# A macaron block on one core: stage 1's small FFN on token halves, one addition moved to GpSimd, and stage 2 entered without a common stop

## The chip, the cores and the metric

One core of a Trainium2 chip runs the whole program in one launch. The metric is the device time of an execution in microseconds (us); lower is better. The core's engines are named as in the profile: PE (TensorE; PEld are its weight loads), DVE (VectorE), ACT (ScalarE), POOL (GpSimd) and SP (SyncE, which here only issues DMAs). Each engine runs its own instruction list in order, and the lists meet at semaphores.

## The reference, cut to what matters

The input `x` is 8192 tokens of 512 features, in float32. Three sub-blocks follow each other, each behind a layer norm.

```python
x = x + 0.5 * ffn(layernorm(x))        # Win, bin, W1, b1, W2, b2, Wout, bout
x = x + attn(layernorm(x))             # rmsnorm, delta-rule attention, rmsnorm, gelu MLP 512-2048-512
x = x + 0.5 * ffn(layernorm(x))        # the same FFN, the same weights

def ffn(x):                            # 512 features -> 64 channels -> 512 features
    s = einsum('btd,dm->btm', x, Win) + bin_
    h = relu(s[..., None] * W1 + b1)   # each of the 64 channels has 16 units of its own
    g = einsum('btmh,mh->btm', h, W2) + b2
    return einsum('btm,md->btd', g, Wout) + bout
```

The attention has 16 heads of 32 features. It is a recurrence over tokens, which the kernel computes in chunks of 32 tokens (a triangular system in each chunk, then a state carried from chunk to chunk).

## The kernel before, in words

The program has three stages, and all engines pass through them in the same order.

**Stage 1** (`pe_project`, `act_project`, `dve_project`, `pool_project`, `sp_project`) handles 16 tiles of 512 tokens. For a tile t it does the first FFN, both norms, and the projections to q, k, v and beta. PE's list in the loop over t is written out by hand: 13 projections `project(t, 0..12)` (j = 0 is beta; then v, q, k for each of four head groups). Between them stand the products of other tiles: `hidden(t + 1)` (Win), `ffn_out(t + 1)` (Wout), the transposes `turn_x(t + 2)` and `turn_h(t + 1)`, and four `gram` products of k and q, two of them of the tile before. The weights of the projections and both sides of them are split into a high and a low part, so that each product is three matmuls (L236 to L238). The FFN's matmuls are plain float32.

The FFN of tile t + 1 runs through the engines as follows. `hidden` (L371) makes s in one PSUM bank. Win's 64 columns stand twice side by side, so that partitions 0 to 63 and 64 to 127 hold the same s. ACT's `relus` (L520) makes 8 units at a time on both halves (units 0 to 7 on the lower partitions, 8 to 15 on the upper ones), 512 tokens wide, in two buffers. DVE's `sums` (L701 for the first, L705 for the other seven) weighs and adds them into `g1`. `ffn_out` (L380) multiplies by Wout, which also stands twice, and so adds the two halves. It writes the banks 6 and 7 in turn, so that its third and fourth matmul wait until DVE's `add_ffn` (L712) has emptied the bank of the first and second. `add_ffn` adds into X, to which DVE's `add_bout` (L693) had added 0.5 bout. Then come the statistics of the second norm (L717, L724), and ACT's second norm.

`system0` is extra work on DVE (L806, L812) and POOL: the triangular systems of the first 1024 tokens are solved inside stage 1, in four parts that go in at t = 3, 6, 9, 12 and come out at t = 6, 9, 12, 15.

SP issues the loads and the stores of a tile in the order of `sp_project`. The stores of k (L270), beta times k (L274) and of the gram results (L283, L286) of the last tile stand at its end.

**Between stage 1 and stage 2** every engine drains and adds to the semaphore `done1`. SP waits for four of them and for all stores, adds the fifth, and only then do all engines go on. SP then issues the first loads of stage 2: `ringA` and `ringB` for four chunks (L1147, L1152, L1158), Wo in four pieces (L1176), and the second system (L1138).

**Stage 2** (`*_delta`) runs over 256 chunks of 32 tokens. Its matmuls are 32x32 tiles (L1245); every four chunks there is one product with Wo (L1330). PE's code begins with straight lines and goes on with a loop. At chunk 0, ACT splits Wo into high and low parts (L1426) after its first chunk's work, DVE makes the low part (L1526), and both then go on. DVE and POOL solve the systems of the 1024 tokens ahead (L1495, L1499) between their other work, in slots that a function hands out at build time.

**Stage 3** (`*_dense`) does the MLP and the second use of the small FFN. There the small FFN is already worked on token halves: `hidden` (L1728) makes tiles of 64 columns, partitions 0 to 63 holding the first half of the tokens and 64 to 127 the second, 16 ReLUs (L1874) and 16 sums (L2020) are 256 wide, and `ffn_out` (L1739) takes 64 rows at a time.

## Time and profile before

| | us |
|---|---|
| median of 3 runs | 3223.64 (3222.89 to 3228.33) |
| the profiled execution, its own time | 3230.83 |
| its span, first to last instruction | 3228.9 |
| mean granted TensorE clock | 0.979 of full |
| PE busy | 3065.5 (95%) |
| DVE busy | 1933.4 (60%) |
| ACT busy | 1420.3 (44%) |
| POOL busy | 1226.6 (38%) |

Shares of busy time are means over the three stages. In the trace, stage 1's projections begin at 52.7 us, the last matmul of stage 1 ends at 937.7, and the first of stage 2 begins at 948.2; stage 3 begins at about 1711. A float32 matmul of L371, L380, L1728 or L1739 shows as two rows of PE, so 4 of them are "x8". The end of a matmul is modelled, and the next one starts before it: the 128x512 matmuls of a projection last 0.39 us each in the rows and follow each other every 0.227 us.

### The profile page before, as it was taken

Reading aid. Unit: us, or ns where it says so; the run is one execution under the profiler, and the core shown is the slowest. Engines: PE = TensorE matmul, PEld = TensorE weight load, DVE = VectorE, ACT = ScalarE, POOL = GpSimd, SP = SyncE. Lnnn points to the kernel's source line nnn. Section 1 sums busy time; section 2 is a strip of 40 time slices with the busy share of each in tenths; the row PEclk is TensorE's granted clock in tenths of the full one; section 3 lists DMA queues with packets and bytes.
Section 4 is the critical chain, followed back from the end, with each engine's and each line's share of the span. In section 5 each row is a group of like instructions: output and inputs, shape, how many; then the busy total and the mean of one; then the engine's idle time right before and its main releaser. Section 6 shows DMA issues by size and latency. Waiting matters only on the chain.

```text
span 3228.9 us, 148563 instructions
## 1 busy us (share of the span) xinstructions
PE 3065.5 (95%) x67876; PEld 2475.0 (77%) x67876; DVE 1933.4 (60%) x3190; ACT 1420.3 (44%) x3226; POOL 1226.6 (38%) x1225
## 2 busy tenths in 40 slices
PE   5999999999957999999999999999999999999998
PEld 3777677676746888888898777777777777777876
DVE  6787878878738888888613434444444444444434
ACT  5544545444413555554454334434433343444334
POOL 1336565655526776766511211212222121222211
PEclk9999999999967999999999999999999999999999
DMA  3545555555465777776672222222222222222220
GB/s 103 158 145 177 145 158 157 154 156 151 145 202 168 217 217 216 217 217 214 194 212 77 65 66 59 72 78 59 72 66 66 74 57 79 66 66 66 79 66 26
DMA packets 471353, 402.34 MB, mean 125 GB/s; under 512 B 68032, under 2 KB 391744, under 8 KB 471104
## 3 DMA queue, kind: packets, MB, share of 16 engines
q1 hardware_dynamic: 460960, 382.39, 40.4%
q10 hardware_dynamic: 10144, 16.63, 1.7%
q8 instruction: 155, 2.54, 0.3%
q14 instruction: 94, 0.77, 0.1%
HBM read 199.69 MB, written 153.09 MB: 109 GB/s over the span
## 4 chain that ended last, share of the span: by engine, by line
PE 59%; DVE 7%; SPq 2%; issue 2%; DMA 1%; ACT 1%; DVEq 0%; ACTq 0%
PE bank L236 14%; PE bank L238 14%; PE bank L237 14%; PE bank L1245 8%; PE bank L1330 6%; DVE tmp L1495 2%; DVE sysf L1499 2%; PE bank L1739 1%; SPq L1667 1%; PE bank L1728 1%; DVE zb L1518 1%; DVE oT_lo L1512 1%; DVE xt L1483 0%; DMA x2T<-HT 0%; DVE sysf L1474 0%
## 5 line engine op out<-in xcount | busy, mean ns | idle before, releaser
L1985 DVE TENSOR_TENSOR glo<-gl,gh 128x512 fp32r<-128x512 f32 x256 | 205.6, 803 | 715.6 <-ACT gh L1857 713.9
L1853 ACT ACTIVATE gl<-bank,b1m 128x512 f32<-128x512 f32 x256 | 175.8, 687 | 712.3 <-PE bank L238 712.3
L238 PE MATMUL bank<-w_hi,glo 128*128 128x512 f32 x1024 | 404.8, 395 | 0.0
L236 PE MATMUL bank<-h,w_hi 128*128 128x512 f32 x1024 | 403.4, 394 | 0.1
L238 PE MATMUL bank<-h,w_lo 128*128 128x512 f32 x1024 | 403.4, 394 | 0.0
L237 PE MATMUL bank<-w_lo,gh 128*128 128x512 f32 x1024 | 402.7, 393 | 0.0
L237 PE MATMUL bank<-h,w_hi 128*128 128x512 f32 x1024 | 402.2, 393 | 0.0
L236 PE MATMUL bank<-w_hi,gh 128*128 128x512 f32 x1024 | 399.8, 390 | 0.0
L1245 PE MATMUL bank<-ringA 32*32 32x32 f32 x16384 | 344.0, 196 | 15.7 <-issue 7.3
L1245 PEld LDWEIGHTS bank<-ringA 32*32 32x32 f32 x16384 | 271.7, 104 | 11.6 <-DMA ringA<-xt 6.2
L1399 ACT ACTIVATE de<-bank 128x64 f32<-128x64 f32 x512 | 114.5, 224 | 301.3 <-PE bank L1245 296.7
L236 PEld LDWEIGHTS bank<-h,w_hi 128*128 128x128 f32 x1024 | 192.3, 188 | 70.9 <-issue 29.0
L237 PEld LDWEIGHTS bank<-w_lo,gh 128*128 128x128 f32 x1024 | 192.0, 188 | 45.5
L237 PEld LDWEIGHTS bank<-h,w_hi 128*128 128x128 f32 x1024 | 192.2, 188 | 44.7
L236 PEld LDWEIGHTS bank<-w_hi,gh 128*128 128x128 f32 x1024 | 192.4, 188 | 44.0
L238 PEld LDWEIGHTS bank<-w_hi,glo 128*128 128x128 f32 x1024 | 192.0, 188 | 42.1
L238 PEld LDWEIGHTS bank<-h,w_lo 128*128 128x128 f32 x1024 | 192.1, 188 | 41.1
L974 POOL TENSOR_TENSOR nrm<-nrm,cst 128x16 f32<-128x16 f32 x64 | 185.5, 2899 | 94.6 <-DVE nrm L768 94.0
L2139 POOL TENSOR_TENSOR Z<-Z,H 128x512 f32<-128x512 f32 x64 | 92.7, 1448 | 293.5 <-DMA H<-x_scratch 293.5
L1499 DVE TENSOR_TENSOR sysf<-sysf,tmp 128x90 f32<-128x90 f32 (+14 forms) x210 | 195.1, 929 | 4.9
L2147 POOL TENSOR_SCALAR rs<-mv 128x4 f32<-128x4 f32 x15 | 8.5, 570 | 481.4 <-DVE mv L2002 481.4
L1245 PE MATMUL bank<-sT,nR 32*32 32x32 f32 x8192 | 184.1, 198 | 6.5 <-issue 6.5
(195 smaller groups left out, 7288.4 us busy)
## 6 DMA issues: line engine op xcount, KB each, us to landing
ringB<-heads_scratch SPq DMA_DIRECT2D x256, 192.0 KB, 3.3
ringA<-heads_scratch SPq DMA_DIRECT2D x256, 128.0 KB, 2.7
x2T<-HT SPq DMA_DIRECT2D x480, 64.0 KB, 2.0
X<-in_L_attn_x SPq DMA_DIRECT2D x16, 1024.0 KB, 10.0
x_scratch<-X SPq DMA_DIRECT2D x16, 1024.0 KB, 4.5
heads_scratch<-vb SPq DMA_DIRECT2D x16, 1024.0 KB, 5.2
heads_scratch<-qk SPq DMA_DIRECT2D x16, 1024.0 KB, 6.8
heads_scratch<-kb SPq DMA_DIRECT2D x16, 1024.0 KB, 5.2
```

What stands on the lines that cost most here:

```text
L236: e.matmul(o, lhs[0], rhs[0], start=first, stop=False)
L237: e.matmul(o, lhs[0], rhs[1], start=False, stop=False)
L238: return e.matmul(o, lhs[1], rhs[0], start=False, stop=last)
L974: e.tensor_tensor(nrm[:, u], nrm[:, u], pos_half.broadcast_to([P, TC]), ALU.pow).then_inc(o_pow, 1)
L1245: made.append(e.matmul(out[r, n, :], lhsT[r, n, :], rhs[r, n, :], start=first and n == 0, stop=True, skip_group_check=True))
L1330: m = e.matmul(bank[B_WO][:, :], oh[x][:, f, :], wo[y][:, f, :], start=k == 0, stop=k == 11)
L1399: e.activation(heads(de[c % 2][:, 2 * h:2 * h + 2, :]), bank[B_DELTA[h]][:, 0:P // 2], ACT.Copy).then_inc(a_delta[c % 4], 1)
L1495: e.tensor_tensor(tt, N[:, :, j + 1:CH, j:j + 1].broadcast_to([P, 3, rows, j]), N[:, :, j:j + 1, 0:j].broadcast_to([P, 3, rows, j]), ALU.m ...
L1499: e.tensor_tensor(N[:, :, j + 1:CH, 0:j], N[:, :, j + 1:CH, 0:j], tt, ALU.add).then_inc(v_sol, 1)
L1853: e.activation(ordered, made, ACT.Gelu_apprx_tanh, bias=b1m[:, m:m + 1]).then_inc(a_gl, 1)
L1985: e.tensor_tensor(gh[k][1][:, :], gl[k][:, :], gh[k][0][:, :], ALU.subtract).then_inc(v_gl, 1)
L2139: e.tensor_tensor(z[:, b, :], z[:, b, :], H[:, b, :], ALU.add).then_inc(o_zx, 1)
```

## The change

1. **The FFN of stage 1 on token halves.** `hidden` makes 8 matmuls of 64 columns by 256 tokens, for each feature block one into partitions 0 to 63 (tokens 0 to 255) and one into 64 to 127 (tokens 256 to 511). `relus` and `sums` take 16 units, each 256 wide, in four buffers of 256. `ffn_out` makes 4 matmuls of 64 rows; they write banks 3, 4, 5 and again 3, for the token blocks 0, 2, 1, 3, so that only the fourth waits for `add_ffn`. The 16 columns of W1, b1, W2 and the one of b2 stand in one tile, `units`.
2. **Places in the loop.** PE does `ffn_out(t + 1)` behind `project(t, 7)` and not ahead of it. DVE does `scale_k(t, 0)` between the third and the fourth `add_ffn`, and `turn_kb(t, 0)` earlier. POOL does `beta_k(t, 0)` ahead of `deviation1(t + 1)`.
3. **bout.** For tiles 2 to 15 `add_bout` is POOL's, at the end of its loop body; DVE keeps the first two tiles.
4. **`h_turned`** waits for the four reads of `project(t, 12)` one by one (`p_hread`) and not for the whole of it.
5. **No common stop.** `done1`, its drains and waits are gone. SP issues the ring loads and Wo before the last tile's stores of v and q (`fill_rings`), and the second system before those of k, beta times k and gram. PE enters stage 2 once the last masks are done, ACT splits Wo ahead of its first chunk, and DVE's tail of stage 1 is in another order.
6. Stage 3 takes `units` as it was folded in stage 1, and loads the eight-column tiles for its last tile.

```diff
@@ hidden, ffn_out
-                    m = e.matmul(bank[WIN_BANK][:, :], win[:, f, :], xT1[:, f, :], start=f == 0, stop=f == NF - 1)
+                    for h in range(2):
+                        r = slice(64 * h, 64 * h + 64)
+                        m = e.matmul(bank[WIN_BANK][r, 0:TOK // 2], win[:, f, r],
+                                     xT1[:, f, h * TOK // 2:(h + 1) * TOK // 2],
+                                     start=f == 0, stop=f == NF - 1, skip_group_check=True)
...
-                e.wait_ge(v_g, 8 * t + 8)
-                for b in range(NB):
-                    bk = 6 + b % 2
+                e.wait_ge(v_g, 16 * t + 16)
+                for i in range(NB):
+                    bk, r = OUT_BANK[i], slice(64 * (i % 2), 64 * (i % 2) + 64)
                     bank_free(bk)
-                    e.matmul(bank[bk][:, :], g1[:, b * P:(b + 1) * P], wout[:, :],
+                    e.matmul(bank[bk][:, :], g1[r, i // 2 * P:(i // 2 + 1) * P], wout[r, :],
                              start=True, stop=True).then_inc(p_wout, 1)
@@ relus
-                    if 8 * t + h >= 2:
-                        e.wait_ge(v_g, 8 * t + h - 1)
-                    e.activation(relu1[h % 2][:, :], bank[WIN_BANK][:, :], ACT.Relu, bias=b1t[:, h:h + 1],
-                                 scale=w1t[:, h:h + 1]).then_inc(a_relu, 1)
+                    if 16 * t + u >= 4:
+                        e.wait_ge(v_g, 16 * t + u - 3)
+                    e.activation(unit_relu(u), bank[WIN_BANK][:, 0:TOK // 2], ACT.Relu, bias=b1u[:, u:u + 1],
+                                 scale=w1u[:, u:u + 1]).then_inc(a_relu, 1)
@@ pool_project
+            def add_bout(t, b):
+                i = t % 2
+                e.wait_ge(a_y0, 4 * t + b + 1)
+                e.tensor_tensor(X[i][:, b, :], X[i][:, b, :], boutb[:, :], ALU.add).then_inc(o_xb, 1)
@@ sp_project, in the last tile
+            def fill_rings():
...
+                for c in range(4):
+                    load_a(c)
+                    load_b(c)
+                e.wait_ge(p_win, NT)
+                e.wait_ge(v_V, 4 * NT)
+                for k in range(NF):
+                    e.dma_start(stage2[k], a["L0_attn_wo"][k * P:(k + 1) * P, :]).then_inc(d_stage[k], 16)
...
+                if t == NT - 1:
+                    fill_rings()
                 store_v(t)
                 store_q(t)
+            e.wait_ge(p_proj, 13 * NT)
+            for quarter in range(4):
+                load_system(1, quarter)
             store_k(NT - 1)
@@ pe_delta
-            e.wait_ge(done1, 5)
+            e.wait_ge(a_ev, 13 * NT)
+            e.wait_ge(v_P, NG * NT)
@@ act_delta
-            e.wait_ge(done1, 5)
+            for k in range(NF):
+                split_wo(k)
```

PE's list around the FFN of the second tile (`project(0, 6)` to `project(0, 7)`): before, the four matmuls of `ffn_out` (L380) stand behind the last matmul of a k projection.

```order
L238 MATMUL bank<-hT_hi,wk_lo 128x512
L380 MATMUL bank<-wout,g 128x512 [waits v_x1,v_g]
L380 MATMUL bank<-wout,g 128x512 [waits v_x1] x3
L236 MATMUL bank<-hT_hi,wv_hi 128x512 [waits a_ev,v_lo]
L237 MATMUL bank<-hT_lo,wv_hi 128x512
```

In the changed kernel the v projection's matmuls come first (L244 to L246 are the three lines of a product in that file), and then `ffn_out` (L448).

```order
L246 MATMUL bank<-hT_hi,wv_lo 128x512
L448 MATMUL bank<-wout,g 128x512 [waits v_lo,v_g]
L448 MATMUL bank<-wout,g 128x512 [waits v_lo]
L448 MATMUL bank<-wout,g 128x512 [waits a_relu]
L448 MATMUL bank<-wout,g 128x512 [waits v_x1]
L244 MATMUL bank<-hT_hi,wq_hi 128x512 [waits a_ev,v_lo]
```

The product moved behind one projection, and of its four waits on `v_x1` one is left, on the fourth matmul; the other three wait for things that are long done there.

DVE's list at the end of stage 1, from the masks of the last `gram(15, 1)` on, before: the two masks come first, and the work that the next gram needs (L764 to L786) behind them.

```order
L795 TENSOR_TENSOR ltb<-bank,cst 128x8x32 [waits d_p,d_lts,p_gram]
L797 TENSOR_TENSOR pb<-bank,cst 128x8x32
L764 STREAM_TRANSPOSE kb<-rawk 128x16x32 [waits o_kb,d_k,a_ev]
L774 TENSOR_SCALAR nrm<-nrm 128x16 [waits o_pow]
L776 RECIPROCAL nrm<-nrm 128x16 [waits v_rn]
L778 TENSOR_TENSOR kb<-kb,nrm 128x16x32 [waits v_rn]
L782 STREAM_TRANSPOSE qk<-kb 128x16x32 [waits p_gram,v_kn]
L768 TENSOR_REDUCE nrm<-sq 128x16 [waits a_sq]
L786 STREAM_TRANSPOSE rawk<-kbuf 128x16x32 [waits o_kb]
```

In the changed kernel (L847 to L859 are the same operations) these come first, and the masks (L868, L870) follow.

```order
L847 TENSOR_SCALAR nrm<-nrm 128x16 [waits o_pow]
L849 RECIPROCAL nrm<-nrm 128x16 [waits v_rn]
L851 TENSOR_TENSOR kb<-kb,nrm 128x16x32 [waits v_rn]
L855 STREAM_TRANSPOSE qk<-kb 128x16x32 [waits p_gram,v_kn]
L837 STREAM_TRANSPOSE kb<-rawk 128x16x32 [waits o_kb,d_k,a_ev]
L859 STREAM_TRANSPOSE rawk<-kbuf 128x16x32 [waits o_kb]
L841 TENSOR_REDUCE nrm<-sq 128x16 [waits a_sq]
L868 TENSOR_TENSOR ltb<-bank,cst 128x8x32 [waits d_p,d_lts,p_gram]
L870 TENSOR_TENSOR pb<-bank,cst 128x8x32
```

What `gram(15, 2)` needs no longer stands behind a wait for `gram(15, 1)`.

## Rows read from the trace of the kernel before

**Rows 1.** The page: busy time by engine, share of the span, instructions.

```profile
PE 3065.5 (95%) x67876; PEld 2475.0 (77%) x67876; DVE 1933.4 (60%) x3190; ACT 1420.3 (44%) x3226; POOL 1226.6 (38%) x1225
```

**Rows 2.** Stretches: us, busy and count of PE, PEld, DVE, ACT, POOL; clock; DMA; GB/s.

```profile
240.00:500.00 260.00, 249.46 (x3378) 187.91 (x3377) 203.96 (x417) 124.37 (x195) 154.66 (x163) 0.99 0.53 159
567.90:574.70 6.80, 5.03 (x6) 2.09 (x7) 4.81 (x8) 0.63 (x1) 3.65 (x5) 0.50 0.44 60
920.00:998.00 78.00, 30.01 (x1488) 25.82 (x1488) 30.00 (x53) 10.84 (x39) 19.32 (x31) 0.50 0.51 158
```

**Rows 3.** Waits of PE, 60 to 905 us: us in total, times, longest.

```profile
PE bank L380 <- DVE g L705: 22.1, 11, 4.1
PE bank L380 <- DVE X L712: 4.8, 12, 0.4
```

**Rows 4.** Timeline of PE, `hidden` of stage 1: start, us, instruction, idle before.

```profile
58.04 3.59 PE L371 MATMUL bank<-xT,win 128*128 128x512 f32 x8
...
61.70 0.39 PE L237 MATMUL bank<-hT_lo,wq_hi 128*128 128x512 f32 x1
```

**Rows 5.** Timeline of PE, `hidden` of stage 3.

```profile
1840.36 1.95 PE L1728 MATMUL bank<-x2T,win 128*64 128x256 f32 x16 [0.80 <-DMA x2T<-HT]
...
1842.57 0.39 PE L237 MATMUL bank<-h,w_hi 128*128 128x512 f32 x1
```

**Rows 6.** Timeline of PE, `ffn_out` of stage 1, in two tiles.

```profile
126.41 1.98 PE L380 MATMUL bank<-wout,g 128*128 128x512 f32 x4
...
130.84 0.40 PE L237 MATMUL bank<-hT_lo,wv_hi 128*128 128x512 f32 x1
...
569.67 6.16 PE L380 MATMUL bank<-wout,g 128*128 128x512 f32 x8 [4.07 <-DVE g L705]
```

**Rows 7.** Timeline of PE, half of `ffn_out` of stage 3.

```profile
1859.04 1.13 PE L1739 MATMUL bank<-wout,HT 64*128 64x512 f32 x4
...
1860.44 0.39 PE L237 MATMUL bank<-h,w_hi 128*128 128x512 f32 x1
```

**Rows 8.** Groups by line and shape: busy us, mean ns, idle before.

```profile
L705 DVE SCALAR_TENSOR_TENSOR g<-relu,w2t,g 128x512 f32<-128x512 f32 x112 | 95.3, 851 | 11.4 <-ACT relu L520 2.0 <-DVE g L705 0.5
L693 DVE TENSOR_TENSOR X<-X,boutb 128x512 f32<-128x512 f32 x64 | 39.5, 675 | 4.6 <-ACT wout L598 4.6
L2161 POOL TENSOR_TENSOR Z<-Z,boutb 128x512 f32<-128x512 f32 x64 | 86.1, 1367 | 18.4 <-ACT H L1863 16.9
L396 PE MATMUL bank<-hT_hi,wb 128*128 128x512 f32 x64 | 30.8, 481 | 0.1
```

**Rows 9.** Timeline of DVE, 256-wide sums of stage 3.

```profile
1850.24 3.42 DVE L2020 SCALAR_TENSOR_TENSOR HT<-HT,w2u 128x256 f32<-128x256 f32 x6
```

**Rows 10.** Timeline of PE, end of stage 1 and start of stage 2.

```profile
919.20 0.50 PE L417 MATMUL bank<-qk,rawk 32*32 32x64 f32 x22 [2.40 <-issue]
924.71 1.76 PE L417 MATMUL bank<-qk,rawk 32*32 32x64 f32 x105 [5.01 <-DVE rawk L786]
...
930.95 1.76 PE L417 MATMUL bank<-qk,rawk 32*32 32x64 f32 x104 [2.82 <-DVE rawk L786]
937.09 0.65 PE L417 MATMUL bank<-qk,rawk 32*32 32x64 f32 x24 [4.38 <-issue]
948.22 1.19 PE L1338 MATMUL bank<-sT 128*128 128x128 f32 x4 [10.49 <-POOL sT L1584]
951.86 1.08 PE L1245 MATMUL bank<-ringA 32*32 32x32 f32 x64 [2.44 <-DMA ringA<-xt_scratch]
```

**Rows 11.** Timeline of DVE, the last mask of stage 1.

```profile
938.65 0.41 DVE L797 TENSOR_TENSOR pb<-bank,cst 128x256 f32<-128x256 f32 x1
```

**Rows 12.** Waits of PE, 905 to 1100 us.

```profile
PE bank L1245 <- issue: 17.4, 8, 2.8
...
PE bank L1330 <- DVE oT_lo L1512: 8.6, 7, 2.1
...
PE bank L1245 <- ACT de L1399: 4.7, 1, 4.7
```

More of the change, by code:

```diff
@@ L837, in dve_project @@
                 e.tensor_copy(wbeta[:, :, 32 * h:32 * h + GROUPS], wbraw[:, :, h:HEADS:4]).then_inc(v_wbc, 1)
-            sums(0, 0, 1, 2, 3, 4, 5, 6, 7)
+            sums(0, *range(16))
             for b in range(NB):
                 add_bout(1, b)
-            add_ffn(0)
+            add_ffn(0, 0, 1, 2, 3)
             for b in range(NB):
@@ L903, in dve_project @@
                 if nxt:
-                    add_ffn(t + 1)
+                    add_ffn(t + 1, 0, 1, 2)
+                scale_k(t, 0)
+                if nxt:
+                    add_ffn(t + 1, 3)
                     for b in range(NB):
@@ L1038, in pool_project @@
                 system0(t, 3)
+                if t + 2 < NT:
+                    for b in range(NB):
+                        add_bout(t + 2, b)
             beta_k(NT - 1, 2)
@@ L1197, in sp_delta @@
                 if i is not None:
+                    if i == 0:
+                        for s in (d_k, d_v, d_q, d_b):
+                            e.wait_ge(s, 16 * NT)
+                        for s in (d_p, d_lts):
+                            e.wait_ge(s, GRAMS * NT)
                     if i >= 2:
```

214 lines of the change are left out of this document (104 added, 110 removed).

## The prediction

> **What bounds the kernel now.** I read the page first: PE is busy for 3065.5 of 3228.9 us, no other engine for more than 60% [rows 1]. So only two things are worth time: work that leaves PE, and moments in which PE stands still. Stage 2 and 3 keep their code and order almost whole, so the gain or loss lies in stage 1 and in the passage to stage 2. The stretches say that stage 1 is PE's: of 260 us PE is busy 249.5, DVE 204 (78%), ACT 48%, POOL 59% [rows 2]. The waits of PE name only one engine there: `ffn_out` waits for DVE's last sum 22.1 us in 11 times, and for `add_ffn` to empty a bank, 12 times 0.4 us [rows 3]. The timeline then gives the length of each FFN product [rows 4, 6], stage 3 the same products in the new form [rows 5, 7], and the end of stage 1 shows a hole of 10.5 us and slow going on both sides of it [rows 10, 12].
>
> All terms are against the profiled execution, span 3228.9 us, own time 3230.8. That is 7.2 us over the median of 3223.64 (0.2%); I take the sum off the median. A change below 0.2% could not be told from none.
>
> **Part 1, hidden.** I measure a product from its start to the second matmul behind it, less the usual 0.227 us between two, since the first one behind is stretched. In stage 1 that is 61.70 - 58.04 - 0.23 = 3.43 us [rows 4]; in stage 3, with 64-column tiles of 256, it is 1842.57 - 1840.36 - 0.23 = 1.98 us [rows 5]. The operands have the same sizes, so the pairs run side by side here too. It saves 1.45 us on PE in each of 15 tiles: **21.8 us**. PE is dense on both sides of `hidden`, so all of it counts.
> The first tile's product runs at 1.2 GHz before the loop, with ACT, DVE and PE in a chain. The product and `ffn_out(0)` save more there, the 16 sums cost some: I put **2.4 us**, between 0 and 5.
>
> The Trainium skill ("TensorEngine Tiling (Array Packing)", Key Properties) says that a change of tiling mode drains TensorE, which speaks against short tiled products between full ones. Stage 3 has exactly such a product between full ones, and its 1.98 us hold what a switch costs; a free switch would not move the sum.
>
> **Part 2, ffn_out.** Before: 130.84 - 126.41 - 0.23 = 4.20 us [rows 6]. In stage 3, two matmuls of 64 rows take 1860.44 - 1859.04 - 0.23 = 1.17 us [rows 7]. Two pairs would be 2.3 us. But the fourth matmul writes bank 3 again and waits for DVE: the first result at about 0.95, the addition (L693's like, 0.68, and two hand-overs) until 1.9, and then 0.9 to 1.0 more: 2.9 us. Where PE had waited for the last sum, DVE still has three operations of about 0.65 to do before its first addition, and the bank comes free at 2.7: 3.6 us. I take 5 tiles at a gain of 1.2 us, 7 at 0.6, and the 3 tiles with a system on DVE, where the product took 6.2 us at a low clock, at 2.0: **16.2 us**. Bounds: 9 (all but those three late) and 28 (both pairs dense).
>
> **Part 3, the wait for the last sum.** Against the end of `hidden`, PE reaches `ffn_out` one projection later: 12 x 0.227 = +2.73 us. DVE's sums get longer. Six 256-wide ones take 3.42 us, 0.57 each [rows 9], so 16 take 9.1; the 8 old ones, with L705 at 0.85 [rows 8] and overlapping a little, 6.8 on the timeline. That is +2.3. The first ReLU is 0.2 shorter. So the wait shrinks by about 0.5 us in each of 10 tiles, less 0.2 where DVE is not quite free when the earlier `hidden` ends: **3.1 us** of the 22.1. The three tiles in which DVE has 4 us of transposes for `system0` keep a wait of 3.5 us. If DVE ran its sums at the 0.49 us they need alone, 1.3 us more per tile would go, about 10 in all; if POOL's load stretches them as L705 (0.75 alone, mean 0.85), another 1 us per tile comes on.
> In such a tile PE's clock fell to 1.2 GHz for 6.8 us, right behind the wait of 4.07 us [rows 2, 6]; in all, three such spells cost some 8.5 us. I count half of it as gone: **4.3 us** (0 to 8.5).
> What is late next: the second norm of tile t + 1. DVE gives its shift about 13 us behind the last sum (it was 14.2), PE needs it 24 us behind (it was 28). It is covered.
>
> **Part 4, h_turned.** The first matmuls of a tile are spaced by DVE's low parts: L396's mean is 481 ns where a dense matmul has 390 [rows 8]. With the reads released one by one, ACT and DVE are ahead by up to 2 us: 4 x 0.09 = 0.36 us per tile, 15 times: **5.4 us** (0 to 5.4).
>
> **Part 5, bout on POOL.** DVE loses 4 x 0.675 = 2.7 us per tile, POOL gets 4 x 1.37 = 5.5 us [rows 8], at the end of its loop body, where it idles for 11 us until the next tile's k. DVE idles in that part too, so the 2.7 us were not on PE's path: **0**. The result is needed a tile later. The chance of harm: POOL's additions run beside the masks and `h_low` of DVE. No `h_low` of the trace has POOL beside it. At the worst it goes like a sum beside POOL's `beta_k`, 1.24 instead of 0.75 us, 4 x 0.5 = 2 us per tile, against the 2 us that part 4 gives as cover.
> The Trainium skill ("SBUF — State Buffer", SBUF: two separate sides) has GpSimd and a DVE instruction with two SBUF inputs exclude each other for whole instructions. By that the sums would suffer and the masks and `h_low`, which read PSUM, would not; the sum stays at 0 by either.
>
> ACT gets 8 more instructions per tile, and its ReLUs take 16 x 0.46 instead of 8 x 0.72 us: +1.6 us at 48% load, hidden behind PE's projections.
>
> **Part 6, the tail of stage 1.** `gram(15, 2)` waited 5.0 us for DVE, and `gram(15, 3)` 2.8 us [rows 10]. In the new order DVE needs no mask before them. Following DVE and POOL through the last products by their durations, `gram(15, 2)` follows `gram(15, 1)` directly at about 919.7 instead of 924.7. POOL's root and `beta_k` put `gram(15, 3)` at about 927. With a code gap like the 4.4 us one (below), the last masks end at about 932.9, not 939.06 [rows 11]: 6.2 us.
> Then the common stop: PE begins stage 2 at 948.2, 9.2 us after the last mask, and waits 2.4 more for the ring's first load [rows 10, 11]. Both go, since the ring is filled some 15 us ahead: 9.2 - 0.2 + 2.4 = 11.4 us. ACT's splitting of Wo behind its own load held PE for 4.7 us [rows 12]; Wo now lands before the masks end. Together 22.3 us.
> Against it: some of PE's stops are "issue", in which it waits for nothing but its own instructions (7.8 us in the last grams with the 2.4 and 4.38 us of rows 10; 17.4 us in 8 stops at stage 2's start) [rows 12]. The longest came while stores were in flight. Now the stores of the last tile, 2 MB of systems, the rings and Wo are under way together. I take 3 us for it, bounds 0 and 12: **19.3 us**.
> The low clock of 78 us around the passage [rows 2] I keep: PE is still more idle than busy there. The 8.6 us that PE waits for `oT_lo` in the first blocks of stage 2 [rows 12] I keep too. DVE's solver work of a block is longer there than PE's, and an earlier start doesn't change this, since its place in DVE's list is tied to PE's chunks.
>
> **Sum.** 21.8 + 2.4 + 16.2 + 3.1 + 4.3 + 5.4 + 0 + 19.3 = 72.5 us. Predicted: 3223.6 - 72.5 = **3151 us**.
>
> **Rivals.**
> *DVE becomes the bound.* A tile of PE's goes from 54 to about 50 us; DVE has some 42 us of work and a chain (ReLU, sums, additions, statistics, norm, transposes, back to `hidden`) of about 47. For it: the sums are longer, POOL is fuller, the waits of rows 3 exist already. Against it: DVE idles 9 to 12 us per tile now. If each tile's wait at `ffn_out` grows by 2 us instead of shrinking, 15 x 2.2 = 33 us are lost: 3184. Chance 0.12.
> *Slower than before.* The clock of PE falls in every tile. What triggers it is a wait like that of 4.07 us [rows 6], with 3.4 us lost behind it [rows 2]. This decides from the point at which the last sum is 4 us late in ordinary tiles, 3.2 more than I work out. In each of 15 tiles it would cost 3.2 + 3.4 us, with the fourth matmul late as well 7.5, or 112 us against 72: 3263. Only contention of POOL far above the one seen speaks for it. Chance 0.03.
> *The passage gives nothing.* PE's code comes in no faster than before and more slowly beside the DMAs; the 19.3 us shrink to 3: 3167. For it: the stops of rows 10 and 12 are already a third of that stretch. Chance 0.12.
> *More than forecast.* The waits at `ffn_out` vanish (another 14 us) and the clock stays at 2.4 GHz in the loop (4 us): 3133. Or the clock falls later in the passage, with the same size. Chance 0.15.
> My forecast: 0.58.
>
> **Range.** The forecast's bounds, the last two rivals and part of the first give 3125 to 3178. Faster by over 0.2% in all cases but the slow one and a remainder: 0.95; within 0.2%: 0.02; slower: 0.03.
>
> **What would show it.** `hidden` at about 2.0 us and `ffn_out` at 2.9 to 3.6 by the same measure; one wait on `add_ffn` per tile; waits for the last sum summing to 15 to 20 us, mostly in three tiles; tiles of 50 us, and stage 1's last matmul near 880; PE's first 32x32 product within 3 us of the last mask, with no stop for Wo. I am wrong if the tiles stay above 52.5 us, if PE waits for DVE in new places (L396 or `gram`), or if the stops by "issue" around the passage sum to over 35 us.

## The result, and the profile after

The changed kernel takes 3180.72 us (median of 4 runs, 3176.48 to 3185.81), against 3225.98 us for the kernel before, run beside it (4 runs, 3222.89 to 3229.53). The ratio is 0.986, interval 0.984 to 0.988: 45 us less, where 72.5 were forecast. The profiled execution has a span of 3180.3 us and took 3182.06 us; its span is 48.6 us shorter than that of the profiled execution before (3228.9), and the tables below, which are cut from these two traces, add up to 48.

The page of the changed kernel, busy time by engine, against [rows 1]:

```profile
PE 3015.1 (95%) x68004; PEld 2473.6 (78%) x68004; DVE 1935.2 (61%) x3262; ACT 1455.8 (46%) x3354; POOL 1274.7 (40%) x1281
```

PE is busy for 50 us less. But its waits have changed their place. The waits of PE in the loop of stage 1, 60 to 905 us, against [rows 3]:

```profile
PE bank L448 <- DVE g L774: 15.1, 11, 3.5
PE bank L487 <- issue: 14.5, 7, 3.6
PE bank L487 <- DVE pb L870: 10.7, 9, 1.9
PE bank L448 <- DVE X L785: 3.2, 8, 0.4
```

L448 is `ffn_out`, and its two waits have shrunk as forecast. L487 is a gram's matmul: it now waits 10.7 us for DVE's masks, in 9 times, which it never did before, and 14.5 us for nothing that the profile shows. These two rows are what this document is about.

The parts that were removed, from the timeline of PE: `hidden` (L437), then `ffn_out` in an ordinary tile and in one in which DVE turns a system.

```profile
57.09 1.95 PE L437 MATMUL bank<-xT,win 128*64 128x256 f32 x16
...
59.30 0.40 PE L245 MATMUL bank<-hT_lo,wq_hi 128*128 128x512 f32 x1
...
499.75 1.98 PE L448 MATMUL bank<-wout,g 64*128 64x512 f32 x6 [0.41 <-DVE g L774]
502.13 1.12 PE L448 MATMUL bank<-wout,g 64*128 64x512 f32 x2 [0.40 <-DVE X L785]
503.18 1.48 PE L487 MATMUL bank<-qk,rawk 32*32 32x64 f32 x128
...
560.61 4.92 PE L448 MATMUL bank<-wout,g 64*128 64x512 f32 x8 [3.52 <-DVE g L774]
```

`hidden` is 59.30 - 57.09 - 0.23 = 1.98 us, as in stage 3 [rows 5]. `ffn_out` with a late sum is 503.18 - 499.75 = 3.43 us, where 3.6 were forecast.

Now the next thing in the same tile, the gram of L487: first PE, then what DVE does in that time.

```profile
510.17 1.03 PE L418 MATMUL bank<-cst,Y 128*128 128x128 f32 x8
512.26 1.42 PE L487 MATMUL bank<-qk,rawk 32*32 32x64 f32 x122 [1.06 <-DVE pb L870]
517.03 0.43 PE L487 MATMUL bank<-qk,rawk 32*32 32x64 f32 x6 [3.35 <-issue]
```
```profile
506.05 0.65 DVE L785 TENSOR_TENSOR X<-bank,X 128x512 f32<-128x512 f32 x1
506.74 2.47 DVE L790 BATCH_NORM_STATS2 stats<-X 128x6 f32<-128x512 f32 x4
509.25 0.38 DVE L797 BATCH_NORM_AGGREGATE mv<-stats 128x2 f32<-128x6 f32 x4
509.55 0.65 DVE L841 TENSOR_REDUCE nrm<-sq 128x16 f32<-128x512 f32 x1
510.12 0.70 DVE L859 STREAM_TRANSPOSE rawk<-kbuf 128x512 f32<-128x512 f32 x1
510.74 0.38 DVE L868 TENSOR_TENSOR ltb<-bank,cst 128x256 f32<-128x256 f32 x1
...
511.71 0.41 DVE L870 TENSOR_TENSOR pb<-bank,cst 128x256 f32<-128x256 f32 x1
```

PE is ready for `gram(t, 0)` at 511.2. It needs banks 6 and 7, which the masks of `gram(t-1, 3)` empty. These stand in DVE's list behind four statistics, the mean, the norms of k and the turn of beta times k, and end at 512.1: a wait of 1.06 us.

The same places in a tile of the kernel before: the start of `ffn_out`, the transposes ahead of `gram(t, 0)` and the gram itself, then DVE's last mask.

```profile
512.67 1.98 PE L380 MATMUL bank<-wout,g 128*128 128x512 f32 x4 [1.11 <-DVE g L705]
526.72 1.03 PE L354 MATMUL bank<-cst,Y 128*128 128x128 f32 x8
527.69 1.48 PE L417 MATMUL bank<-qk,rawk 32*32 32x64 f32 x128
```
```profile
524.62 0.41 DVE L797 TENSOR_TENSOR pb<-bank,cst 128x256 f32<-128x256 f32 x1
```

From the start of `ffn_out` to the end of the last mask it is 12.4 us in both kernels (525.03 - 512.67 and 512.12 - 499.75). So DVE has not become slower there. But from the same start to the point at which PE is ready for the gram it was 15.0 us, and is 11.5 now (511.20 - 499.75). Of these 3.5 us, 2.7 are the twelve matmuls of `project(t, 7)`, which point 2 of the change put ahead of `ffn_out`; the rest is the shorter `ffn_out`. A slack of 2.7 us became a wait of 1.06.

Then the gram runs for 122 of its 128 matmuls and stops for 3.35 us. In three tiles (297.7, 517.0 and 738.0 us) there is such a stop of 3.64, 3.35 and 2.63 us, and each time the clock falls to 1.2 GHz for 6.8 us at once. Three more spells of low clock, 23.9 us together, stand behind the three waits of 3.5 us for the last sum. The stretches, against [rows 2]; the second is the low clock behind the first of these stops, the third the passage:

```profile
240.00:500.00 260.00, 245.82 (x3439) 192.35 (x3439) 209.96 (x442) 143.37 (x247) 176.55 (x189) 0.97 0.55 163
296.80:303.60 6.80, 5.93 (x22) 4.50 (x23) 1.12 (x2) 0.81 (x3) 5.84 (x6) 0.52 0.50 143
900.00:978.00 78.00, 41.85 (x2510) 37.14 (x2510) 36.30 (x55) 17.32 (x68) 22.24 (x36) 0.61 0.66 201
```

The passage, from the timeline of PE, against [rows 10] (L1390 and L1297 are stage 2's first lines), with DVE's last mask, against [rows 11]:

```profile
905.59 0.64 PE L487 MATMUL bank<-qk,rawk 32*32 32x64 f32 x22 [4.28 <-issue]
908.23 1.75 PE L487 MATMUL bank<-qk,rawk 32*32 32x64 f32 x105 [2.00 <-DVE rawk L859]
913.27 0.65 PE L487 MATMUL bank<-qk,rawk 32*32 32x64 f32 x23 [3.28 <-issue]
915.34 1.20 PE L1390 MATMUL bank<-sT 128*128 128x128 f32 x4 [1.43 <-issue]
916.47 1.08 PE L1297 MATMUL bank<-ringA 32*32 32x32 f32 x64
```
```profile
914.83 0.41 DVE L870 TENSOR_TENSOR pb<-bank,cst 128x256 f32<-128x256 f32 x1
```

The stop of 10.5 us between the stages is gone, as forecast. The waits of PE, 905 to 1100 us, against [rows 12]:

```profile
PE bank L1297 <- issue: 24.0, 10, 5.3
PE bank L1382 <- DVE oT_lo L1561: 8.9, 9, 2.1
PE bank L487 <- issue: 7.6, 2, 4.3
```

**Where the time went.** I cut both traces at the same instructions: the first `hidden` of the loop, the last one, the last gram, the first 32x32 product of stage 2, its first product with Wo, the first dense matmul of stage 3.

| stretch | before | after | change |
|---|---|---|---|
| to the first hidden | 58.0 | 57.1 | -1 |
| 14 loop tiles | 770.6 | 753.4 | -17 |
| last hidden to last gram | 108.8 | 103.2 | -6 |
| to the first 32x32 product | 14.4 | 2.9 | -11 |
| to the first Wo product | 40.8 | 42.9 | +2 |
| rest of stage 2 | 722.2 | 719.2 | -3 |
| stage 3 | 1509.8 | 1497.4 | -12 |

The 14 loop tiles alone, each of PE's groups measured from the last dense matmul ahead of it to the second behind it, waits included. "Low" is the time at 1.2 GHz in them; the last two rows are experiments, below.

| | hidden | ffn_out | first products of a tile | turns | grams | other products | sum | low |
|---|---|---|---|---|---|---|---|---|
| before | 48.1 | 88.1 | 33.7 | 51.8 | 88.5 | 460.5 | 770.6 | 17 |
| after | 29.5 | 68.2 | 27.4 | 62.0 | 100.2 | 466.1 | 753.4 | 44 |
| masks before statistics | 31.2 | 68.4 | 28.5 | 52.1 | 104.6 | 460.6 | 745.4 | 27 |
| ffn_out early | 31.5 | 115.5 | 27.3 | 51.9 | 88.6 | 473.0 | 787.7 | 92 |

The three terms that the change attacks gave 18.6 + 19.9 + 6.3 = 44.8 us. Of that, 10.2 came back in front of a gram (seven waits for the masks, 7.8 us together, end a group of turns), 11.7 in the grams and 5.6 in the dense products, by the clock. So stage 1's loop gave 17 us. And stage 3, whose code is the same but for some small tables, gave 12 us that nobody had counted.

### The profile page after: what moved, and what is told of

It is laid out like the page before. It is cut to its first block, busy times and chain, and to the rows that moved or that the text cites. A ratio compares the mean times of both kernels' runs of the same rounds, so it can differ in the third digit from the quotient of the medians.

```text
span 3180.3 us, 149246 instructions
## 1 busy us (share of the span) xinstructions
PE 3015.1 (95%) x68004; PEld 2473.6 (78%) x68004; DVE 1935.2 (61%) x3262; ACT 1455.8 (46%) x3354; POOL 1274.7 (40%) x1281
## 4 chain that ended last, share of the span: by engine, by line
PE 67%; DVE 17%; issue 6%; SPq 4%; DMA 2%; ACT 2%; POOL 1%; DVEq 0%; ACTq 0%; POOLq 0%
PE bank L244 15%; PE bank L246 14%; PE bank L245 14%; PE bank L1297 9%; PE bank L1382 6%; SPq L1714 4%; DVE g L774 3%; DVE sysf L1548 2%; DVE tmp L1544 2%; PE bank L487 2%; DMA x2T<-HT 2%; DVE stats L742 1%; PE bank L1786 1%; PE bank L1775 1%; PE bank L427 1%
## 5 line engine op out<-in xcount | busy, mean ns | idle before, releaser
L244 PE MATMUL bank<-h,w_hi 128*128 128x512 f32 x1024 | 404.7, 395 | 0.1
L246 PE MATMUL bank<-h,w_lo 128*128 128x512 f32 x1024 | 400.4, 391 | 0.0
L246 PE MATMUL bank<-w_hi,glo 128*128 128x512 f32 x1024 | 399.7, 390 | 0.0
L244 PE MATMUL bank<-w_hi,gh 128*128 128x512 f32 x1024 | 399.5, 390 | 0.0
L1297 PE MATMUL bank<-ringA 32*32 32x32 f32 x16384 | 344.5, 197 | 12.8 <-issue 8.7
L1297 PEld LDWEIGHTS bank<-ringA 32*32 32x32 f32 x16384 | 272.1, 105 | 11.0 <-issue 6.0
L244 PEld LDWEIGHTS bank<-h,w_hi 128*128 128x128 f32 x1024 | 192.1, 188 | 67.6 <-issue 29.0
L246 PEld LDWEIGHTS bank<-h,w_lo 128*128 128x128 f32 x1024 | 192.2, 188 | 40.8
L244 PEld LDWEIGHTS bank<-w_hi,gh 128*128 128x128 f32 x1024 | 192.2, 188 | 40.3 <-DVE glo L2031 0.5
L246 PEld LDWEIGHTS bank<-w_hi,glo 128*128 128x128 f32 x1024 | 192.2, 188 | 40.1
L1297 PE MATMUL bank<-sT,nR 32*32 32x32 f32 x8192 | 184.4, 198 | 8.8 <-issue 8.7
```

Of the source, the lines that this page charges most:

```text
L244: e.matmul(o, lhs[0], rhs[0], start=first, stop=False)
L246: return e.matmul(o, lhs[1], rhs[0], start=False, stop=last)
L1297: made.append(e.matmul(out[r, n, :], lhsT[r, n, :], rhs[r, n, :], start=first and n == 0, stop=True, skip_group_check=True))
```

## The experiments

Each ratio is against the kernel before, run on the same chip at the same time. The kernel before took 3221.7 to 3226.0 us on these occasions, so a difference of two medians from different occasions carries some 4 us; where it matters, the difference of the ratios is given too (0.001 is 3.2 us).

**1. DVE's masks earlier** (`masks_first`), on the changed kernel:

```diff
-                norms(t, 1)
-                turn_kb(t, 0)
                 if t:
                     mask(t - 1, 6)
                     mask(t - 1, 7)
+                norms(t, 1)
+                turn_kb(t, 0)
```

> The changed kernel with the last two masks of a tile (of gram(t-1, 3)) ahead of the norms and the turn of beta times k in DVE's list, not behind them. Theory A, gram(t, 0) waits for the banks that these masks empty: the wait of about 1.1 to 1.4 us goes in the ordinary tiles (8.8 us for the mask in all falls below 3, and no wait on the turned beta times k comes in its place), some low-clock spells behind the gram go too, the loop is 9 to 15 us shorter, about 3168 us against 3180. The stops by issue in the middle of gram(t, 0) stay, since the stores still begin just there. Theory B, DVE is simply behind in its whole list (its longer sums bound the loop): the wait moves to the turned beta times k, the time stays at 3178 to 3182.

Measured: 3170.99 us, ratio 0.9846 (0.9832 to 0.986), 10 us less than the changed kernel by the medians and 4.5 by the ratios, whose intervals overlap. The wait for the masks fell from 10.7 to 2.9 us, but 12.3 us (9 times) now stood against the turned beta times k. Both theories had a part: the loop is 6 us shorter in the trace, and DVE's list behind `ffn_out` is what PE waits for, not the masks alone.

**2. The masks ahead of the statistics** (`masks_before_stats`), DVE's list from the fourth `add_ffn` on; also `norms(t, 0)` stands ahead of `turn_kb(t-1, 3)`:

```diff
                     add_ffn(t + 1, 3)
+                if t:
+                    mask(t - 1, 6)
+                    mask(t - 1, 7)
...
+                    stats_x1(t + 1, 0)
+                    stats_x1(t + 1, 1)
+                turn_kb(t, 0)
...
                     mean1(t + 1)
                 norms(t, 1)
-                turn_kb(t, 0)
-                if t:
-                    mask(t - 1, 6)
-                    mask(t - 1, 7)
```

> The changed kernel with DVE's list behind the fourth add_ffn in the order in which PE's next gram needs it: the two last masks of gram(t-1, 3), two statistics, the turn of beta times k, the other statistics, mean, norms; and the norms of k ahead of the turn of beta times k of the tile before. Theory A (gram(t, 0) waits for what stands behind the statistics in DVE's list): the turned operand is there 2.5 to 3 us earlier than with the masks moved alone, the waits of PE at this gram (12.3 + 2.9 us with the masks moved) fall below 3 us, in all about 10 us less than the 3171 of that run: 3161 us. Rival, the stores of the masks then begin 2.5 us earlier and lie beside all of the gram, the stops for code grow by what the waits lose: 3170 us.

Measured: 3166.08 us, ratio 0.983 (0.9817 to 0.9843): 14.6 us less than the changed kernel by the medians, 9.7 by the ratios; the 14 loop tiles are 8 us shorter. The waits of PE in it, 60 to 905 us:

```profile
PE bank L487 <- issue: 17.2, 13, 2.7
PE bank L448 <- DVE g L774: 15.7, 11, 3.6
PE bank L487 <- DVE rawk L859: 4.0, 1, 4.0
...
PE bank L487 <- DVE pb L870: 2.9, 1, 2.9
```

The two waits of the gram for DVE that are left are one each, at the end of stage 1. The tile shown above in this version: DVE's last mask starts at 503.20, and PE finds its banks free.

```profile
507.31 1.43 PE L487 MATMUL bank<-qk,rawk 32*32 32x64 f32 x122
510.18 0.31 PE L487 MATMUL bank<-qk,rawk 32*32 32x64 f32 x6 [1.44 <-issue]
```

So the wait goes when the masks come 4.7 us earlier in DVE's list. That it also goes with DVE's list as it is, when `ffn_out` stands in its old place, is experiment 4. The stops without a releaser didn't go: they are 17.2 us in 13 times, mostly short.

**3. The gram one projection later** (`gram_later`):

```diff
-                gram(t, 0)
                 project(t, 10)
                 if t + 2 < NT:
                     turn_x(t + 2, 2)
                     turn_x(t + 2, 3)
+                gram(t, 0)
```

> The changed kernel with PE's gram(t, 0) behind project(t, 10) and the two turns of x that follow it; DVE's list as it is. Theory A: PE arrives 4 us later at the gram, the wait for the masks is gone in all tiles, and the stores of the gram before it have run 4 us longer, so fewer of its instructions are fetched beside them: gaps in the first gram of a tile fall from about 25 us over the loop to under 10, low clock in the loop from 44 to under 30 us, about 3162 us. Rival, the fetch stops belong to the density of the gram's instructions and not to the stores: they stay (about 13 us in stops over 1.2 us), only the wait of 9 us goes: about 3170. Theory B (DVE bound): the wait turns up at the next tile's first products or at gram(t, 1), 3180.

Measured: 3193.97 us, ratio 0.9911 (0.9898 to 0.9925), 13 us slower than the changed kernel. The wait for the masks is gone, but the turns in front of the gram wait for ACT to empty their bank (8.6 us, 9 times), and 29.0 us of stops by issue stand in the loop, up to 3.9 us long, now also in dense products right behind a gram. Both of my theories were wrong here: a later gram is no remedy for the stops.

**4. ffn_out in its old place** (`ffn_early`):

```diff
-                project(t, 7)
                 if t + 1 < NT:
                     ffn_out(t + 1)
+                project(t, 7)
```

> The changed kernel with ffn_out(t+1) back ahead of project(t, 7). Theory A: PE reaches the last sum 2.7 us earlier, the wait for it grows from 15 to 40 or 45 us over the loop, and since PE is then later at gram(t, 0), the wait for the masks (8.8 us) goes: about 3196 us. Theory B (DVE bounds the loop, wherever PE waits): the loop keeps its length, 3180 us.

Measured: 3215.99 us, ratio 0.998 (0.997 to 0.999). The wait for the last sum, 60 to 905 us:

```profile
PE bank L448 <- DVE g L774: 50.4, 14, 6.1
PE bank L487 <- issue: 4.9, 3, 2.2
```

The wait was 5 to 10 us longer than I gave it, and the clock was low for 92 us of the loop, in spells of 3 to 14 us behind waits of 2.2 to 6.1 us. This is the rival "slower than before" of the prediction nearly come true: with `ffn_out` in its old place the whole gain of the FFN's short products is eaten. The grams, which PE then reaches late, are back at 88.6 us, and none waits for the masks: from the start of `ffn_out` PE has at least 14.3 us to `gram(t, 0)` again in every tile that has these masks, and they end within 13.0. So the place of `ffn_out` is what took the slack from the masks.

**5. The stores held back** (`stores_later`): SP issues a tile's gram stores only when PE has done `gram(t, 0)` of the next.

```diff
                 e.wait_ge(v_lt, NG * t + NG)
+                if t < NT - 1:
+                    e.wait_ge(p_gram, NG * (t + 1) + 2)
```

> The changed kernel with SP's stores of a tile's grams held back until PE has done gram(t, 0) of the next tile. Theory, the long stops of PE in the middle of this gram (3.6, 3.4, 2.6 us) are its code fetched behind the packets of these stores: these three stops shrink below 1.3 us, with them the low clock behind them, 10 to 15 us of the loop; against it the masks of gram(t, 0) may come later, since they wait for these stores: about 3172 us. Rival, the stops belong to the gram's dense instructions alone: they stay at 2.6 to 3.6 us, and the time is 3180 or more.

Measured: 3188.19 us, ratio 0.9898 (0.9883 to 0.9913). In the tiles of the long stops of 3.64 and 3.35 us, where no stores are in flight now:

```profile
301.69 0.31 PE L489 MATMUL bank<-qk,rawk 32*32 32x64 f32 x8 [1.99 <-issue]
...
520.61 0.31 PE L489 MATMUL bank<-qk,rawk 32*32 32x64 f32 x6 [1.98 <-issue]
```

The same matmuls stop, for 2.0 us: the stores made 1.4 to 1.7 us of them, not the whole. In the tile of the third stop, of 2.63 us, no stop is longer than 0.4 us. By the forecast of this run they were to shrink below 1.3 us. The cost that I had named was larger: the masks of the next grams wait for these stores, and the grams wait 18.7 us for masks.

**6. The code moved by half a block** (`code_shifted`):

```diff
             e.wait_ge(d_cst, 16)
+            for _ in range(64):
+                e.transpose(bank[2][:, 0:P], ident, ident)
             for f in range(NF):
```

> The changed kernel with 64 unused transposes at the start of PE's list, some 128 instructions or half of what one code fetch of the trace brings (16 KB). Theory, a stop by issue falls where the end of a fetched block lies inside a gram, and lasts longer with stores in flight: the stops of 3.64, 3.35 and 2.63 us are no longer in these tiles, others of 1 to 3.6 us stand elsewhere, the ordinary tiles keep their waits of 1.1 to 1.4 us for the masks, and the total changes by up to 8 us either way, with 2 us more at the start. Rival, the stops belong to the place in the tile (stores beside the gram) whatever the code's place: the same three stops in the same tiles, 3182 us.

Measured: 3178.76 us, ratio 0.9858 (0.9844 to 0.9872). The three stops are gone from their tiles, and the long ones stand in other tiles:

```profile
194.73 0.44 PE L487 MATMUL bank<-qk,rawk 32*32 32x64 f32 x9 [3.65 <-issue]
...
631.10 0.43 PE L487 MATMUL bank<-qk,rawk 32*32 32x64 f32 x5 [3.65 <-issue]
```

So the tile is picked by the place of the code. The stops are fetches of PE's code: the trace has a queue of its own for it (q8), with packets of 16,384 bytes. Where PE is held up by one packet after the other, from 903 to 929 us, it does 127 or 128 matmuls and as many weight loads from the start of one packet to the next. For each of the seven stops of the changed kernel between 225 and 890 us such a packet starts, and PE goes on 2.2 to 2.8 us later, though the packet itself takes 0.9 to 1.3 us. One of them, 230.9 to 232.3 us, had the DMA engines for itself, and the stop of the gram there was 1.43 us; another, 514.8 to 515.8, lay beside 82 packets of stores, and that is the stop of 3.35 us. There PE had been standing for 1.1 us when the packet started (1.2 us at the stop of 3.64, 0.3 at that of 2.63); at the four stops of 1.2 to 1.4 us the packet had started 1.0 to 1.5 us before PE stopped. So the long stops are those whose packet started late, and the time from its start is the same. The DMA queues in these two windows:

```profile
q8 instruction: 1, 0.02, 5.9%
```
```profile
q1 hardware_dynamic: 82, 0.24, 82.9%
q8 instruction: 1, 0.02, 5.9%
```

The Trainium skill ("Advanced Engine Details and Errata", ISA Cache) has code come in lines of 16 KB or 256 instructions. The packets agree in both: 16,384 bytes, and the 127 or 128 matmuls with as many loads. A gram is 128 matmuls and as many weight loads, so as much as one packet brings, and PE runs through it in 1.26 us (median), faster than the 2.2 us in which a line arrives.

**7. The masks and the late ffn_out, at two places of the code** (`masks_before_stats_late_out`, `masks_shifted`, `late_out_shifted`). The first has `ffn_out` behind `project(t, 8)` in the five tiles in which DVE turns a system; the others are experiment 2 and this one with the 64 transposes.

```diff
                 project(t, 7)
+                late = group_in(t) is not None or group_out(t) is not None
+                if late:
+                    project(t, 8)
                 if t + 1 < NT:
                     ffn_out(t + 1)
                 if t:
                     gram(t - 1, 3)
-                project(t, 8)
+                if not late:
+                    project(t, 8)
```

> The same, and in the tiles in which DVE turns a system (five of them) ffn_out(t+1) behind project(t, 8). Theory A: the waits of 3.5 us for the last sum in these tiles fall to 0.8 us, and the low clock behind them (6.8 us a time, 3.4 us lost) goes; DVE is late in these tiles by its own work, so some 1 to 2 us come back at gram(t, 0): 10 us less than the run before it, 3151 us. Theory B (DVE's list bounds these tiles): the wait moves whole to gram(t, 0), no change.

> The version with masks before statistics, with 64 unused transposes at the start of PE's list, which move its code by half a fetched block. Theory: of its 17.2 us of stops by issue in 13 grams a different set appears, between 8 and 25 us in sum, so 3158 to 3175 us; no wait on the masks. Rival, the stops are tied to the grams and the stores: the same 17 us in the same tiles, 3168 us.

> The version that also has ffn_out late in the system tiles, code moved by half a block. It had 28.7 us of stops for code against 17.2 and so gained nothing over its base. Theory: with other block ends the stops come back towards 12 to 18 us and the 10 us of waits that it saves show: 3152 to 3162 us. Rival, the late ffn_out itself brings the stops (the gram and the turns come in one stretch): 3168 us again.

Measured: 3168.53 us (ratio 0.9817 to 0.9855), 3174.75 (0.9825 to 0.9855) and 3170.75 (0.9811 to 0.9838). The waits of PE for the last sum in the first of them did fall, and the loop has only 10 us of low clock:

```profile
PE bank L487 <- issue: 28.7, 17, 3.3
PE bank L448 <- DVE g L778: 6.4, 10, 1.0
PE bank L418 <- ACT xT L574: 4.4, 3, 1.5
```

But the stops for code rose from 17.2 to 28.7 us and took most of the gain (the 14 loop tiles take 742.5 us against 745.4). With the code moved they were 19.2 and 26.5 us: other tiles, nearly the same sums. So the place of the code picks the tile, and for the late `ffn_out` the rival holds: the order of the work has most of the sum. Two places of the code are few, though, and `early_pad` of experiment 11, with the same lists as experiment 2, had 21.6 us. None of the three is better than experiment 2; their intervals overlap.

**8. bout on DVE** (`bout_on_dve`), and no `add_bout` on POOL:

```diff
@@ DVE's list
                 turn_v(t, 2)
+                if nx2:
+                    for b in range(NB):
+                        add_bout(t + 2, b)
                 turn_k(t, 2)
```

> The changed kernel with all of add_bout on DVE again, where it stood before. By the forecast it costs DVE 2.7 us a tile in a part where it idles, and nothing on PE's path: 3178 to 3184 us. Rival, POOL's additions slow DVE's masks and h_low at the end of the tile: then it gets faster, by up to 2 us a tile, 3155 us, and the mean of the first matmuls of a tile (the beta group) falls. Third, DVE is fuller than I count: 3190 to 3200.

Measured: 3179.9 us, ratio 0.9872 (0.9857 to 0.9887): no difference that can be told. The move to POOL was worth nothing, as forecast, and POOL's additions harm nobody that PE waits for.

**9. h_turned as before** (`hread_undone`):

```diff
-                elif t and f < NF - 1:
-                    e.wait_ge(p_hread, (NF - 1) * (t - 1) + f + 1)
-                elif t:
+                elif t and f == 0:
                     e.wait_ge(p_proj, 13 * t)
```

> The changed kernel with h_turned waiting for the whole of project(t, 12) again. The first matmuls of a tile (beta group, 27.4 us in 14 tiles) go back to 33.7 us. If that counts in full: 3187 us. Rival, PE then comes later to gram(t, 0) and the wait for the masks shrinks by what the start of the tile costs: 3181 us.

Measured: 3184.54 us, ratio 0.9871 (0.9856 to 0.9886). The first products of a tile went back to 33.2 us, 5.8 us more, and the time rose by some 4 us, with an error of the same size; the wait for the masks did not shrink (11.2 us). In the trace the loop is 2.7 us longer. So the stretch is shortened as forecast; how much of it counts in the time isn't shown, since the intervals overlap and the low clock in the loop was another one too (27 us against 44).

**10. The passage** (`passage_only`: point 5 of the change made on the kernel before; `common_stop`: undone in the changed kernel). The core of the first:

```diff
@@ pe_delta
-            e.wait_ge(done1, 5)
+            e.wait_ge(a_ev, 13 * NT)
+            e.wait_ge(v_P, NG * NT)
@@ sp_project
+                if t == NT - 1:
+                    fill_rings()
```

> The kernel before with only the passage changed: no common stop, the rings, Wo and the second system ahead of the last stores, DVE's tail in the new order. FFN, bout, and the small tables as before. By the forecast 19.3 us less, 3203 us; by the trace of the changed kernel, in which the stretch from the last hidden to stage 2's first Wo product is 15.1 us shorter, 3207 us. Rival, the passage gives nothing by itself and the gain there came with the new place of the tables: 3219 us or more.

> The changed kernel with the passage of the kernel before: the common stop, the rings and Wo behind it, DVE's old tail. Forecast of the passage: 19.3 us, so 3200 us; by the two traces 15.1 us, 3196 us; by the passage alone on the kernel before 10 us, 3191 us.

Measured: 3213.35 us, ratio 0.9962 (0.9951 to 0.9973), so 12 us less by the ratio; and 3188.95 us, ratio 0.9885 (0.987 to 0.990), so 8 us more than the changed kernel. From the last hidden to the first Wo product the traces say 14.2 and 13.8 us. The passage is worth 8 to 14 us, not 19.3.

**11. The place of the tables** (`placed`; `arena_moved`; `early_pad` on experiment 2).

```diff
@@ placed: the kernel before
+        units = sbuf(top, "units", [P, 64])
+        w1u, b1u, w2u, b2u = units[:, 0:16], units[:, 16:32], units[:, 32:48], units[:, 48:49]
...
-        w1u = sbuf(top, "w1u", [P, 16])
...
@@ arena_moved: the kernel before
         b2u = sbuf(top, "b2u", [P, 1])
+        sbuf(top, "pad", [P, 8])
```

> The kernel before with nothing but the place of the small tables changed: W1, b1, W2 and b2 for the units stand early in SBUF as they do in the changed kernel, so that all tiles behind them move by 256 bytes. Theory, the place of the operands sets the cadence of dense matmuls: stage 3 becomes 11 us shorter (mean spacing of its dense matmuls 227.5 and not 231.4 ns), about 3214 us. Rival, the 11 us of stage 3 were chance or come from another edit: 3226 us, stage 3 as long as before.

> The kernel before with 32 unused bytes ahead of the tiles that only stage 2 and stage 3 have; w1, h and all tiles of stage 1 keep their addresses. In the kernel whose small tables were moved, w1 and h had moved by 256 bytes and these later tiles (w2, gh, the ring) by 32. Theory, it is their place modulo 64 bytes: stage 3 is 14 us shorter here too, about 3208 us. Rival, it is the 256 bytes or where w1 and h stand: nothing changes, 3222 us. A part of each: something between.

> The version with masks before statistics, with 32 unused bytes early in SBUF, so that nearly all tiles of all stages change their place modulo 64 bytes, back to where gh and w2 stood in the kernel before; w1, h and the projections' weights then stand at a multiple of 64, which they never did. Theory, gh and w2 at a multiple of 64 bytes are slow: stage 3 gets 14 us back, 3180 us. Rival, what counts is that w1, h and gh, w2 stand alike modulo 64 (they differed in the kernel before and agree in the changed one): stage 3 stays short, 3166 us. Stage 1's products show by the way whether its weights' place matters: no change expected.

Measured: 3208.2 us, ratio 0.9961 (0.9948 to 0.9974); 3208.34, ratio 0.995 (0.9937 to 0.9964); 3171.37, ratio 0.9835 (0.9822 to 0.9848). Stage 3 took 1495.1, 1496.1 and 1495.6 us, against 1509.8. The same 1250 us of stage 3 (1850 to 3100) in the kernel before, with 32 unused bytes ahead of its late tiles:

```profile
1850.00:3100.00 1250.00, 1246.67 (x5521) 996.50 (x5520) 552.50 (x897) 506.60 (x864) 253.11 (x199) 1.00 0.26 69
```

PE gets through 5521 matmuls there; the kernel before has 5473 in the same row. In four of the six kinds of pairs one dense matmul follows the other at 227 ns, where it was 230 to 234. By the sizes of the tiles in the order in which they are allocated, in the kernel before w1 and h start 32 bytes past a multiple of 64 and w2, gh and all of stage 3's own tiles at a multiple; in the three others all of them start alike, at 32 past in two and at a multiple in the last. So it is not that a multiple of 64 is slow: `early_pad` has it everywhere, and is fast. That the two groups stand alike is what the three fast ones share; why this matters was not tried. That `early_pad` is 5 us slower than experiment 2 by the medians (1.6 by the ratios, which do not tell them apart) fits stage 1's loop, 10 us longer in the trace with more stops (23.2 us) and 10 us more of low clock; whether its own tiles' place has a part in it stays open.

## Why the prediction was wrong, step by step

- **Part 1, hidden:** right. 1.98 us a product, 18.6 us in 14 tiles where 14 x 1.45 = 20.3 were forecast. To the first hidden 1 us, not 2.4.
- **Parts 2 and 3, ffn_out and its waits:** right in sum: 19.9 us in 14 tiles, where 14/15 of 16.2 + 3.1, or 18.0, were forecast. The wait for the last sum went from 22.1 to 15.1 us, with 3.5 us in each of three tiles; sums take 0.54 us, within what was given.
- **Part 3, "What is late next":** this step failed. I counted the projection that PE now does ahead of `ffn_out` as 2.73 us gained at the last sum, and followed only DVE's next norm, which I found covered by 11 us. I did not follow what else stands behind the sums: the masks that empty the banks of `gram(t, 0)`, and beta times k. The same 2.73 us are missing between `ffn_out` and this gram (15.0 us became 11.5), and DVE needs 12.4 to 12.7: it was 1.1 to 1.4 us late there in five ordinary tiles and 0.8 in two. These seven waits are 7.8 us, and the turns with them are 10.2 us longer; the sum had nothing for it. Experiment 2 moved only DVE's order, and experiment 4 only `ffn_out`; with either the wait is gone, and experiment 2 brought 10 to 15 us.
- **Part 3, the clock:** half of 8.5 us was to go. Instead the low clock rose from 17 to 44 us. The spells behind the three waits for the last sum did not shrink (17.1 us before, 23.9 after), and 20.5 us came behind the stops inside the gram; the dense products took 5.6 us longer.
- **Stops by issue in the loop:** no term at all. I had priced them for the passage only. 5.8 us in the loop became 16.5. Experiments 5 and 6 show what they are: lines of code that arrive later than a gram uses them up.
- **Part 4, h_turned:** 6.3 us of the stretch where 5.4 were forecast; undone, it changed the time by some 4 us with an error of the same size.
- **Part 5, bout:** right, by experiment 8; it clears the rival in which POOL makes DVE the bound by contention, as far as `add_bout` goes. The harm that I allowed for, an `h_low` slowed like a sum from 0.75 to 1.24 us, isn't there: in the changed kernel 44 of the 60 `h_low` have POOL beside them and take 0.75 us like the others.
- **Part 6, the passage:** 5.6 us ahead of the last gram, where 6.2 were forecast, and 11.5 for the common stop, as worked out (11.4). But the stops by issue grew from 25.2 to 33.0 us, 8 us where 3 were given (bounds 0 to 12), and the 4.7 us of Wo do not show in the time. From the last `hidden` to the first product with Wo it is 15 us less, where 19.3 were forecast.
- **Not seen:** 12 us in stage 3 from the place of the small tables (14 to 15 in the three runs of experiment 11), in the diff as one line. This is luck: without it the changed kernel would have missed by some 42 us and not by 30.
- **In sum:** the terms for the loop come to 48 us in 14 tiles, and it gave 17; the passage gave 15 of 19; stage 3 gave 12 of nothing.
- Of my rivals, "DVE becomes the bound" came nearest in time (3184) and half in mechanism: DVE's order, not its load, and at the gram, not at `ffn_out`. Its sign of "PE waits for DVE in new places (L396 or `gram`)" is what the profile shows; tiles stayed above 52.5 in the mean (53.8 us).

What is open: why the sum of the stops for code is 6.7 us in the loop with `ffn_out` early, 16.5 in the changed kernel, and 11 (`masks_first`), 19 (experiment 2) and 29 to 30 (late `ffn_out`) with fewer waits. Mostly they rise as PE waits less for DVE, which would fit a fetch that needs PE's pauses, but `masks_first` does not fit, and `gram_later`, with 29.0 us, shows that the order alone can do it too. How far ahead PE's code is fetched was not tried.

The best version that ran is experiment 2, at 3166.08 us: 0.983 of the kernel before, and faster than the changed kernel by 14.6 us by the medians, 9.7 by the ratios. The two versions with the late `ffn_out` can't be told from it.

## What to carry to other kernels

When the engine that bounds a loop gets shorter, list everything that it waits on in one round with the slack of each, bank releases too, and not only the next link of the chain that was shortened. Work that is moved ahead of a wait is taken from the slack of everything behind it: here 2.7 us of slack were given away with one projection, and 1.1 to 1.4 were lacking. Price the stops without a releaser like any other wait, above all at dense small matmuls, and see what the clock does behind them. And when a tile moves in SBUF, all behind it move: hold the addresses still, or time the move alone, before a gain in untouched code is put down to the change.

## What was not expected of the hardware

- 32 bytes of padding made 1250 us of dense matmuls 0.9% faster (5473 to 5521 in the same time); moving the small tables did the same. Stage 1's loop, whose tiles all moved by 256 bytes in `placed`, stayed as it was (770.6 and 773.0 us).
- A gram of 128 matmuls of 32x64 took 1.26 us; PE went on 2.2 to 2.8 us after the packet with its next line of code had started, also with no other packet in flight. Over all runs, the stops of 0.9 us and more with no other packet in flight were 1.0 to 2.0 us long, those beside other packets 0.9 to 3.9 us.
- In the changed kernel the clock fell to 1.2 GHz for 6.8 us right behind the stops of 2.63 to 3.64 us inside a gram, and stayed at 2.4 GHz behind those of 1.2 to 1.4 us. It fell in nearly every tile of `ffn_early`, behind waits of 2.2 to 6.1 us. Between the two it went either way: behind the stops of 1.98 and 1.99 us of `stores_later` it fell for 3.4 us, and behind one of 3.05 us in `code_shifted` it did not fall.
